# Splitting the second-half q.k dot products of a slab into two f16 parts in a fused attention and feed-forward kernel

## The reference, cut to what matters

```
x = x + 0.5 * ffn(layernorm(x))
x = x + attn(layernorm(x))          # attn adds its own input again
x = x + 0.5 * ffn(layernorm(x))

ffn(x):  h = silu(x @ w1.T * s1) * (x @ w2.T * s2)      # 256 -> 1024, ternary weights
         h = gelu(h @ h1.T * t1); h = gelu(h @ h2.T * t2)   # 1024 -> 1024
         return h @ w3.T * s3                              # 1024 -> 256

attn(x): q, k, v, beta = split((layernorm(x) * g + b) @ w_qkvb + b_qkvb), beta = sigmoid(beta)
         k = k / max(|k|, 1e-6)                            # per head
         for t in time:                                    # S: 16 x 16 per head
             S = S + outer(beta_t * (v_t - S k_t), k_t)
             o_t = S q_t
         return x + o @ w_out + b_out
```

## Time and profile before

| | |
|---|---|
| median of 3 runs | 2029.9 us (2028.86 to 2032.04) |
| the profiled execution | 2030.32 us |
| its span, first to last instruction | 2028.6 us |
| mean granted TensorE clock | 0.963 |
| PE busy | 1843.0 us, 91% |
| POOL busy | 1270.3 us, 63% |
| DVE busy | 1221.9 us, 60% |
| ACT busy | 878.3 us, 43% |

### The profile page before, as it was taken

One profiled execution on the slowest core, in us unless ns is written; L12 is line 12 of the kernel. 1 busy time (PEld: TensorE's weight loads), 2 busy tenths in 40 slices (PEclk: granted clock), 3 DMA queues, 4 the chain that ended last, 5 costly groups with the idle time before them and its releaser, 6 DMA issues.

```text
span 2028.6 us, 30162 instructions
## 1 busy us (share of the span) xinstructions
PE 1843.0 (91%) x8610; PEld 953.6 (47%) x8610; DVE 1221.9 (60%) x3381; ACT 878.3 (43%) x1480; POOL 1270.3 (63%) x1409
## 2 busy tenths in 40 slices
PE   5997777999999999999999999999999999788879
PEld 2444443455544544455544555455544555444424
DVE  4127874567746775567746776467756666576610
ACT  4463222545363453545354353534454453342152
POOL 5365543677747685677836795677846785384543
PEclk9999878999999999999999999999999999798989
DMA  6200000000000000000000000000000000000000
GB/s 208 88 1 1 1 1 0 1 1 2 1 23 1 1 1 15 9 2 1 1 23 1 2 1 1 22 2 1 1 11 1 1 1 1 11 1 1 1 11 11
DMA packets 4512, 23.48 MB, mean 12 GB/s; under 512 B 609, under 2 KB 609, under 8 KB 2785
## 3 DMA queue, kind: packets, MB, share of 16 engines
q1 hardware_dynamic: 4320, 21.26, 3.1%
HBM read 17.06 MB, written 4.19 MB: 10 GB/s over the span
## 4 chain that ended last, share of the span: by engine, by line
PE 56%; POOL 14%; DVE 13%; issue 13%; ACT 3%; POOLq 0%; DVEq 0%; DMA 0%; ACTq 0%; SPq 0%
PE ffn_bank L1002 36%; POOL hid_lo L511 5%; POOL hid L520 4%; PE att_bank L1045 4%; PE att_bank L1035 4%; DVE state_bank L859 3%; DVE terms L857 3%; PE state_bank L1053 2%; PE ffn_bank L985 2%; PE att_bank L1023 2%; PE ln_bank L954 2%; DVE NK L806 2%; POOL pairs L543 2%; PE att_bank L1062 1%; DVE roots L743 1%
## 5 line engine op out<-in xcount | busy, mean ns | idle before, releaser
L1002 PE MATMUL ffn_bank<-hid_hi,w_sb 128*128 128x512 f16 x2304 | 888.5, 386 | 16.6 <-ACT hid L635 11.3
L1002 PE MATMUL ffn_bank<-hid_lo,w_sb 128*128 128x512 f16 x2304 | 887.8, 385 | 0.0
L511 POOL TENSOR_TENSOR hid_lo<-hid,hid_hi 128x512 f16<-128x512 f32 x384 | 445.9, 1175 | 326.1 <-ACT hid_hi L619 325.9
L543 POOL TENSOR_TENSOR pairs<-KQ 128x32 f32<-128x32 f32 (+14 forms) x496 | 324.4, 665 | 116.4 <-PE att_bank L1035 69.8
L1002 PEld LDWEIGHTS ffn_bank<-hid_hi,w_sb 128*128 128x128 f16 x2304 | 238.0, 103 | 274.0 <-issue 26.6
L1002 PEld LDWEIGHTS ffn_bank<-hid_lo,w_sb 128*128 128x128 f16 x2304 | 228.4, 99 | 252.7 <-issue 33.4
L648 ACT ACTIVATE hid<-ffn_bank,par_sb 128x512 f32<-128x512 f32 x256 | 161.8, 682 | 411.1 <-PE ffn_bank L1002 401.6
L619 ACT CAST hid_hi<-hid 128x512 f16<-128x512 f32 x384 | 224.3, 620 | 114.1 <-POOL hid L520 114.1
L859 DVE TENSOR_REDUCE state_bank<-terms 128x8 f32<-128x16 f32 (+14 forms) x960 | 226.8, 236 | 33.0
L550 POOL TENSOR_TENSOR pairs_lo<-pairs,pairs_hi 128x32 f16<-128x32 f32 (+15 forms) x248 | 170.2, 687 | 121.0 <-ACT pairs_hi L671 111.7
L520 POOL TENSOR_TENSOR hid<-hid,gate 128x512 f32<-128x512 f32 x128 | 164.7, 1287 | 108.6 <-ACT hid L635 108.6
(11 more groups left out here) (92 smaller groups left out, 2079.7 us busy)
## 6 DMA issues: line engine op xcount, KB each, us to landing
NK<-in_w SPq DMA_DIRECT2D x11, 1024.0 KB, 4.8
X<-in_x SPq DMA_DIRECT2D x8, 512.0 KB, 3.6
out<-X SPq DMA_DIRECT2D x8, 512.0 KB, 2.9
wqkvb_sb<-in_wqkvb SPq DMA_DIRECT2D x1, 1024.0 KB, 4.8
wout_sb<-in_wout SPq DMA_DIRECT2D x1, 256.0 KB, 5.1
par_sb<-in_par SPq DMA_DIRECT2D x1, 24.0 KB, 1.8
```

What stands on the lines that cost most here:

```text
L511: pool.tensor_tensor(hid_lo[layer % 2][:, m, :], hid[:, u % 3, :], hid_hi[layer % 2][:, m, :], ALU.subtract).then_inc(hid_lo_ready, 1)
L543: pool.tensor_tensor(packed(pair(pairs, q), w), later, half(KQ[:, 0, :], h)[:, :, :, 0:w], ALU.mult).then_inc(pairs_made if is_split(q) el ...
L1002: mm = nc.tensor.matmul(ffn_ps(off, j), weight(name, kk, 2 * pair + i), v[:, kk, :], start=kk == 0 and part == 0, stop=kk == KT_FF - 1 and ...
```

## The change

The 16 products of a slab's second-half q.k rows, numbers 46 to 61, are split too. Two lines change. SPLITS goes from 31 to 47.

```
-SPLITS = DOT_QK[1] - DOT_KK[1]
+SPLITS = DOTS - DOT_KK[1]
...
 def is_split(q):

-    return DOT_KK[1] <= q < DOT_QK[1]
+    return q >= DOT_KK[1]
```

## The result

The kernel after the change takes 2051.4 us (median of 5 runs, 2044.05 to 2055.97) against 2029.9 us before (5 runs, 2026.81 to 2032.04). The ratio is 1.0103, 95% interval 1.008 to 1.0125: slower by about 1%, 21 us. Forecast were 2048 us, 2037 to 2060.

What follows compares the result with a forecast made beforehand. PE set the pace before the change, POOL would after it in the second-half q.k stretch. 7.3 us for slabs 1 to 6, 4.8 and 5.6 for slabs 0 and 7 make 17.7 on 2030.3: 2048 us, range 2037 to 2060.

Steps and rivals of the forecast that it cites:

- The sum: Whole kernel: 7.3 us for six full slabs plus 4.8 and 5.6 for slabs 0 and 7, 17.7 us slower.
- POOL becomes the bound: Second-half q.k stretch: POOL's 15.12 us and 10.9 of new subtractions make 26 us, more than the stretch's 21.5.
- Full slabs: Slabs 1 to 6: POOL's work delays dot 61, each slab 1.2 us longer, 7.3 us for six.
- its fixed part: Slab 1: POOL's work up to the end of two hid_lo subtractions at 530.04 us; 23.0 us follow to subtraction 61.
- Slabs 0 and 7: Slabs with one FFN call beside the attention: POOL delays the output projection by 4.8 and 5.6 us.
- Rival (c), the holes cost clock: PE's wait before dot 55 lowers its clock: 0 to 1.6 us per full slab, up to 10, 2058 us; 20%.
- Casts, DVE and the f32 wait at nothing: ACT's 128 casts, DVE's unchanged work and POOL's dropped wait for an f32 dot four before: no time cost.
- Rival (a), POOL keeps up: PE saves 3.7 us in slabs 1 to 6, about 1 each in slabs 0 and 7: 2006 us; 5%.
- (b): A standoff: full slabs gain or lose nothing, the two single ones lose less, 2030 to 2034 us; 5%.
- (d): The change doesn't do what it says; excluded beforehand, as all four engines read is_split.

Runs made afterwards that it cites:

- A fourth, with 4 ticks: The changed kernel, but POOL makes the products of dots 46 to 61 4 ticks ahead instead of 6; 2121.6 us, ratio 1.047.
- the run with narrow casts: The changed kernel, but ACT's casts for dots 46 to 61 cover only 32 columns; 2050.3 us, ratio 1.0103.
- the run with the doubled dots: The changed kernel, but PE does each split dot of 46 to 61 twice over into the same bank; 2056.3 us.

## Why the prediction was right

**The sum.** Forecast 17.7 us, and the stretches, which are what it summed, grew by 22.8. That 2048 came within 3.4 us of the measured time is in part luck, as the pieces outside the stretches happened to be 1.8 us shorter in the profiled execution.

**POOL becomes the bound.** Right, and shown by three runs from different sides: less work on POOL turns the loss into a gain, more work on PE mostly vanishes, less on ACT changes nothing. A fourth, with 4 ticks, shows the condition: the products must be early enough.

**Full slabs.** Forecast 1.2 us per slab, measured 1.72 in slabs 1 to 3 and 1.6 to 1.7 in the rest. The step was that POOL needs 23.0 us from its fixed part to subtraction 61; it took 23.35 (768.84 to 792.19). Of the 0.35 us, 0.29 is a wait that the sum had only for slabs 0 and 7: subtraction 49 stands behind the cast of 49, which waits for dot 46, in the full slabs too. Another 0.13 us is the hand-over from POOL to PE before dot 59 (subtraction 59 ends at 790.01, the dot starts at 790.14), which the sum had at nothing. The mechanism was right and the term was small by a third. The prediction also let narrow split dots cost a few tenths over half, by their weight load. They don't: from 770.07 to 770.12 PE does both matmuls of the 32-column dot, 0.05 us. It was of no weight, as PE doesn't set the pace.

**Slabs 0 and 7.** Forecast 4.8 and 5.6 us, measured 6.8 and 5.9. From the state update to the end of subtraction 61 slab 0 was forecast to take 22.6 us (318.5 less 295.93, where the update started before) and took that. The rest, from there to the projection, took 5.3 us where 3.4 were forecast. Windows of slab 0 in the changed kernel:

```profile
303.00:314.50 11.50, 4.84 (x22) 1.58 (x22) 6.67 (x14) 3.71 (x7) 11.50 (x14) 0.98 0.00 0
314.60:321.40 6.80, 6.44 (x17) 2.44 (x18) 4.21 (x8) 2.40 (x4) 4.73 (x5) 0.53 0.00 0
317.06:322.41 5.35, 4.81 (x14) 1.61 (x13) 3.97 (x6) 2.12 (x4) 2.27 (x3) 0.64 0.00 0
```

PE is busy for 4.8 of 11.5 us, as each dot waits for POOL, and then the clock falls to 1.2 GHz just where PE has to finish the last three dots. The last line is the piece from the end of subtraction 61 to the projection. The same piece in the run with narrow casts and in the run with the doubled dots:

```profile
314.71:318.87 4.16, 2.33 (x10) 0.90 (x10) 4.00 (x5) 1.20 (x3) 2.27 (x2) 1.00 0.00 0
```

```profile
318.43:322.97 4.54, 3.08 (x15) 1.19 (x13) 3.99 (x6) 1.57 (x3) 2.27 (x2) 1.00 0.02 4
```

At the full clock it takes 4.2 us, and with twice the dot work still only 4.5. So of the 1.9 us that were missing 1.2 or more go with the clock, and up to 0.7 would be missing without it. In the narrow-cast run those are DVE's: it is still at work on dot 60 when dot 61 is done and starts on that one 0.96 us after the dot's start, not 0.63 as the sum had, and its closing sum (L888 there) took 1.67 us and not 1.26. Why that sum was longer is open. The narrow-cast run's stretch was 26.02 us; its other 0.8 us less than 27.97 lie before the end of subtraction 61. Slab 7 took 23.2 us to the end of subtraction 61, 23.5 forecast, and 3.9 behind it, 3.3 forecast.

**Rival (c), the holes cost clock.** Its first half came true, its price did not. The hole before dot 55 was forecast at about 2 us and is 2.50. Windows of two slabs in the changed kernel, first the hole, then what follows it, slab 4 and slab 2:

```profile
1247.30:1249.80 2.50, 0.01 (x1) 0.02 (x2) 0.11 (x1) 0.00 (x0) 2.50 (x4) 0.91 0.00 0
1249.90:1253.30 3.40, 3.40 (x11) 1.38 (x11) 1.46 (x3) 1.01 (x2) 3.40 (x5) 0.58 0.00 0
780.10:782.60 2.50, 0.02 (x1) 0.00 (x0) 0.14 (x1) 0.04 (x1) 2.50 (x4) 1.00 0.00 0
782.60:786.00 3.40, 2.64 (x12) 1.01 (x12) 2.03 (x4) 1.10 (x2) 3.40 (x5) 1.00 0.00 0
```

The same hole is followed by the low clock in slab 4 (also in 5 and 6) and not in slab 2 (nor in 1 and 3). Yet the stretch is 29.03 us with it and 29.05 without. PE has slack exactly there, so a slow PE only fills its own waits. The lower bound of "0 to 1.6" was the value in the full slabs. In slab 0, where the fall meets the end of the stretch, it did cost, as said above; the prediction had no term for that.
The rule of the Trainium skill (TensorE: Matmul & The Clock Gate, What's actually happening), that an idle TensorE is put back to 1.2 GHz, agrees in three of these six holes, and in the full slabs its price was nil.

**Casts, DVE and the f32 wait at nothing.** Right in the full slabs once the products lead by 6 ticks. The prediction had "a cast has a tick to spare", which is the order's doing; its bound for ACT, 0.6 us once in a slab, was far too small for an order without that spare, where the casts cost 8.6 us a slab. In the first slab DVE's work on dot 60 showed for some tenths, as above.

**Rival (a), POOL keeps up.** Excluded. The forecast said that the 15 subtractions would have to cost 6 us and not 10.9 for a gain of 3.7 us; narrowed to 32 columns, with 7 us less on POOL, they gave 2.9.

**Rivals (b) and (d).** Excluded. The lowest of the five runs took 2044.05 us, where a standoff would be 2030 to 2034. L1035 has 240 records instead of 496, and L550 has 376 instead of 248, so the change does what it says.

## What to carry to other kernels

When a change moves work off the engine that sets the pace, add the moved work to what the receiving engine does in that stretch, not to its share of the whole run: POOL was at 63% of the kernel, but at 15.1 of 21.5 us here with 10.9 to come. A saving that halves one engine's cost is worth only what the next engine leaves, and then the right amount of it is a part: in the six full slabs, splitting every second dot won 12 us where splitting all 16 lost 8. Where one part of a kernel has less work beside it, like the first and last slab here, cost it by itself, since it gave more than half of the loss.

## What the runs showed of the hardware that was not expected

The granted clock is a chance from run to run in this kernel. The run with the split in slabs 1 to 6 has times from 2030.0 us at a mean granted clock of 0.968 to 2043.95 us at 0.960, with one and the same program. A hole in PE's work of 2.5 us is followed by the low clock or is not. Where PE sets the pace afterwards, a fall costs what it takes away: a piece between two full slabs' stretches, PE busy for 95% of it, took 203, 204.6 or 206.3 us at a mean clock of 1.00, 0.99 or 0.98. Where another engine sets the pace it costs nothing: 29.03 us at 0.94 and 29.05 at 1.00 for the stretch.
